# Fused gated cross-attention and attention block on one core: who issues the transfers that build the key stack

## What is computed

```
def reference(x, ctx, g_xattn, g_ffn, Wa, Wp, w_std, w_rec):
    xq = quant_dequant_act_1x128(layernorm(x))
    wq = quant_dequant_weight_128x128(ctx)
    x = x + tanh(g_xattn[0]) * einsum('emk,enk->emn', xq, wq)
    fused = layernorm(x) @ (Wa * col_scale)          # Q, K (32 columns a head), V
    scores = einsum('bhtd,bhsd->bhts', Qf, Kf) * scale, causal
    y = einsum('bhts,bhsd->bhtd', softmax(scores), V)
    return x + tanh(g_ffn[0]) * (y @ Wp)
```

## Time and profile before

| | us |
|---|---|
| median of 3 runs (513.59 to 514.74) | 514.0 |
| the profiled execution | 513.52 |
| its span, first to last instruction | 511.5 |
| TensorE busy, 87% of the span | 443.2 |
| VectorE busy, 65% | 331.8 |
| ScalarE busy, 53% | 273.6 |
| GpSimd busy, 28% | 145.2 |

### The profile page before, as it was taken

One profiled execution on the slowest core, in us unless ns is written; L12 is line 12 of the kernel. 1 busy time (PEld: TensorE's weight loads), 2 busy tenths in 40 slices (PEclk: granted clock), 3 DMA queues, 4 the chain that ended last, 5 costly groups with the idle time before them and its releaser, 6 DMA issues.

```text
span 511.5 us, 7890 instructions
## 1 busy us (share of the span) xinstructions
PE 443.2 (87%) x2536; PEld 319.0 (62%) x2536; DVE 331.8 (65%) x1110; ACT 273.6 (53%) x530; POOL 145.2 (28%) x264
## 2 busy tenths in 40 slices
PE   0366886999878999999888999999788999999995
PEld 0244665776544788776555788776455788666763
DVE  4789624588997243688998243678995255565535
ACT  2886226687446542687455552588556333454430
POOL 5667435233214300233214400233222101121110
PEclk9999998999999999999989999999999999999999
DMA  6402154414420244314420244414310243332102
GB/s 227 184 1 84 42 186 97 104 37 99 104 78 1 63 104 140 119 36 100 102 86 3 53 97 120 143 38 99 89 27 2 69 101 88 93 96 72 55 9 82
DMA packets 28024, 42.61 MB, mean 83 GB/s; under 512 B 8272, under 2 KB 8528, under 8 KB 27984
## 3 DMA queue, kind: packets, MB, share of 16 engines
q1 hardware_dynamic: 26448, 41.97, 29.4%
q10 hardware_dynamic: 1536, 0.14, 0.2%
HBM read 12.59 MB, written 4.19 MB: 33 GB/s over the span
## 4 chain that ended last, share of the span: by engine, by line
PE 57%; DVE 15%; ACT 12%; SPq 6%; DMA 4%; issue 2%; POOL 2%; ACTq 1%; POOLq 0%; DVEq 0%
PE pv_bank L731 8%; PE mm_bank L579 7%; PE mm_bank L581 7%; PE mm_bank L580 7%; PE exp_bank L717 5%; SPq L387 5%; DVE x_all L1205 5%; PE max_bank L700 4%; DVE max_bank L1234 4%; ACT work L1005 3%; PE mm_bank L758 2%; PE mm_bank L759 2%; PE mm_bank L760 2%; PE turn_bank L595 2%; DMA col_root<-in_L_ffn_w_rec 2%
## 5 line engine op out<-in xcount | busy, mean ns | idle before, releaser
L1234 DVE CUSTOM_DVE_ANT_0 max_bank<-max_bank,causal 128x512 f32<-128x512 f32 (+3 forms) x256 | 118.9, 516 | 46.9 <-PE max_bank L700 46.9
L495 POOL TENSOR_SCALAR_AFFINE_SELECT work<-work 128x384 f32<-128x384 f32 x64 | 33.5, 524 | 285.4 <-ACT work L1005 285.4
L1005 ACT ACTIVATE work<-exp_bank 128x512 f32<-128x512 f32 (+1 forms) x192 | 91.5, 525 | 39.9 <-PE exp_bank L717 39.5
L731 PE MATMUL pv_bank<-work,v_aug 128*33 128x256 f32 (+3 forms) x512 | 75.2, 436 | 0.0
L700 PE MATMUL max_bank<-k_stack,q_stack 96*128 96x512 f32 (+3 forms) x256 | 61.7, 336 | 12.0 <-DVE row_max L1234 6.0
L717 PE MATMUL exp_bank<-q_stack,k_stack 97*128 97x512 f32 (+3 forms) x256 | 66.5, 351 | 3.6 <-DMA q_stack<-neg_max 1.9
L1217 DVE SCALAR_TENSOR_TENSOR qk_lo<-mm_bank,col_root,qk_hi 128x512 fp32r<-128x512 f32 x32 | 24.0, 749 | 61.3 <-ACT qk_hi L978 61.2
L1205 DVE SCALAR_TENSOR_TENSOR x_all<-mm_bank,coef,x_all 128x128 f32<-128x128 f32 x224 | 60.4, 340 | 2.5 <-PE mm_bank L627 2.5
L700 PEld LDWEIGHTS max_bank<-k_stack,q_stack 96*128 96x128 f32 x256 | 45.3, 192 | 22.7 <-DVE row_max L1234 10.1
L731 PEld LDWEIGHTS pv_bank<-work,v_aug 128*33 128x33 f32 x512 | 27.4, 110 | 47.2 <-issue 40.4
L717 PEld LDWEIGHTS exp_bank<-q_stack,k_stack 97*128 97x128 f32 x256 | 43.7, 191 | 16.2 <-ACT work L1005 4.3
(11 more groups left out here) (161 smaller groups left out, 794.1 us busy)
## 6 DMA issues: line engine op xcount, KB each, us to landing
q_stack<-qk_hi SPq DMA_DIRECT2D x128, 64.0 KB, 2.0
k_stack<-qk_hi SPq DMA_DIRECT2D x128, 64.0 KB, 2.0
x_all<-in_x SPq DMA_DIRECT2D x16, 256.0 KB, 4.1
ctx_raw<-in_ctx SPq DMA_DIRECT2D x16, 256.0 KB, 3.8
q_stack<-qk_lo SPq DMA_DIRECT2D x64, 64.0 KB, 2.0
k_stack<-qk_lo SPq DMA_DIRECT2D x64, 64.0 KB, 2.0
out<-x_all SPq DMA_DIRECT2D x16, 256.0 KB, 2.2
work<-in_L_ffn_Wa SPq DMA_DIRECT2D x3, 768.0 KB, 9.4
```

What stands on the lines that cost most here:

```text
L495: pool.affine_select(out=three, in_=three, compare_op=ALU.is_ge, fill=0.0, base=0, pattern=[[0, 3], [1, P]], channel_multiplier=-1)
L731: last = pe.matmul(pv_bank[64 * j:64 * j + D + 1, P * m:T], v_aug[:, m, 2 * u + j, :], prob[j][:, PROB_COL[m]:PROB_COL[m] + T - P * m], st ...
L1005: act.activation(prob[j][:, UNIT_COL[k]:UNIT_COL[k] + UNIT_LEN[k]], exp_bank[(3 * j + k) % 2][:, 0:UNIT_LEN[k]], ACT.Exp, scale=SCALE).the ...
L1234: last = dve.tensor_tensor_reduce(max_bank[unit % 2][:, col:col + width], max_bank[unit % 2][:, col:col + width], causal[:, T - width:T], ...
```

## The change

SyncE keeps the six transfers of each step that build the query stack. The six that build the key stack are issued by GpSimd from a new function `stack_k`, with a semaphore per slot of their own, `s_kstack`; both engines use a common helper `stack_rows`. TensorE and ScalarE, which waited for 192 counts of `s_stack`, wait for 96 of each. GpSimd's calls stand at fixed places of its program: four in `POOL_FIRST`, step 4's at the head of step 2, step 5's behind step 2's zeroing, those of steps 6 and 7 behind step 3's, and the four for the next batch at the batch's end. Nothing of the arithmetic changes.

```
-POOL_FIRST = "i0 s0 s1 s2 s3 o0 s4 s5 s6 l0 l1 s7 l2 l3 r0 j0 j1 j2 r1 j3 g0 g1 g2 g3 p0"
+POOL_FIRST = "i0 s0 s1 s2 s3 o0 s4 s5 s6 l0 l1 s7 l2 l3 r0 j0 j1 j2 r1 j3 k0 k1 g0 g1 g2 k2 k3 g3 p0"
...
+K_STACKS = {2: (5,), 3: (6, 7)}
...
+        s_kstack = [sem(f"s_kstack{i}") for i in range(SLOTS)]
...
+        def stack_rows(eng, u, w, dst, parts, done):
+
+            g, s = u // 2, u % SLOTS
+            for j in range(2):
+                rows = slice(D * (2 * (u % 2) + j), D * (2 * (u % 2) + j) + D)
+                for a, part in enumerate(parts):
+                    eng.dma_start(dst[D * a:D * a + D, s, j, :].bitcast(FP32),
+                                  part[rows, g % 2, w, :].bitcast(FP32)).then_inc(done[s], 16)
...
-                for dst, w, parts in ((q_stack, 0, (qk_hi, qk_lo, qk_hi)), (k_stack, 1, (qk_hi, qk_hi, qk_lo))):
-                    sp.wait_ge(s_qklo, 8 * n + 2 * g + w + 1)
-                    for j in range(2):
-                        rows = slice(D * (2 * (u % 2) + j), D * (2 * (u % 2) + j) + D)
-                        for a, part in enumerate(parts):
-                            sp.dma_start(dst[D * a:D * a + D, s, j, :].bitcast(FP32),
-                                         part[rows, g % 2, w, :].bitcast(FP32)).then_inc(s_stack[s], 16)
-
+                sp.wait_ge(s_qklo, 8 * n + 2 * g + 1)
+                stack_rows(sp, u, 0, q_stack, (qk_hi, qk_lo, qk_hi), s_stack)
...
+            def stack_k(n, u, first=False):
+
+                if not first:
+                    pool.wait_ge(s_st, 48 * n + 6 * (u - SLOTS) + 6)
+                pool.wait_ge(s_qklo, 8 * n + 2 * (u // 2) + 2)
+                stack_rows(pool, u, 1, k_stack, (qk_hi, qk_hi, qk_lo), s_kstack)
...
+                elif kind == "k":
+                    stack_k(0, i, first=True)
...
                 for u in range(STEPS):
+                    if u == 2:
+                        stack_k(b, 4)
                     fill(POOL_GAPS[u][0])
                     zero_future(b, u, 0)
                     fill(POOL_GAPS[u][1])
                     zero_future(b, u, 1)
+                    for v in K_STACKS.get(u, ()):
+                        stack_k(b, v)
                     fill(POOL_GAPS[u][2])
+                if more:
+                    for v in range(SLOTS):
+                        stack_k(n, v)
...
-                    pe.wait_ge(s_stack[s], 192 * (2 * n + u // SLOTS + 1))
+                    pe.wait_ge(s_stack[s], 96 * (2 * n + u // SLOTS + 1))
+                    pe.wait_ge(s_kstack[s], 96 * (2 * n + u // SLOTS + 1))
...
-                        act.wait_ge(s_stack[s], 192 * (2 * n + g // 2))
+                        act.wait_ge(s_stack[s], 96 * (2 * n + g // 2))
+                        act.wait_ge(s_kstack[s], 96 * (2 * n + g // 2))
```

## The result

| | us |
|---|---|
| median before, measured alongside (4 runs, 512.93 to 514.74) | 513.8 |
| median after (4 runs, 547.02 to 555.63) | 552.1 |
| ratio, 95% interval | 1.066, 1.062 to 1.071 |
| the profiled execution after; its span | 548.9; 546.8 |

The ratio leaves disturbed runs out, so it lies nearer to the profiled execution than the median does; 1.0664 of 513.8 is a loss of 34 us. The direction held, and the range (547 to 655) by 1 us, since 1.0664 of 513.8 is 547.9. The forecast of 605 did not: it had the loss at 91.6 us, more than twice the measured one.

What follows compares the result with a forecast made beforehand. TensorE held 57% of the chain of waits, SyncE's queue 6%. Terms of 19.4 + 55.2 + 7.0 + 4.0 + 6 = 91.6 us added to 513.5 gave 605 us, range 547 to 655.

Steps and rivals of the forecast that it cites:

- c = 1.0: Assumed price in us of one transfer issue on GpSimd; the sum moves by 120 us per us of it.
- rival 1: An issue on GpSimd costs what it costs SyncE, 0.635 us; 562 us in all, chance 0.19.
- start: Batch 0's start: twelve issues delay g0, twelve more delay g3, its cast and step 0's negation; +19.4 us.
- step 2: Batches 0 to 2: six issues for step 4 stand ahead of scaling u0, delaying ScalarE's cast; +7.7 us each.
- step 3: Batches 0 to 2: step 5's transfers sit between causal zeroing and u2, whose cast already waited; +6.0 us each.
- step 4: Batches 0 to 2: 12 issues, r0 and two zeroings come before TensorE's weighted values; +4.7 us each.
- last batch: Twelve issues and two zeroings end after TensorE needs them, with short steps not covering the issues; +4.0 us.
- batch ends: After g3, six issues and a landing finish later than TensorE reads that stack; +3.5 us, twice.
- the clock: Six idle times of 6 to 8 us at steps 2 and 3 each bring slow clock costing about 1; +6 us.
- Rival 2: Issuing on GpSimd is nearly free, up to 0.4 us an issue; 520 to 545 us, chance 0.07.
- Rival 3: GpSimd's issues are held up by VectorE, an issue costing above 1.4 us; 725 us at 2.0, chance 0.07.
- Rival 4: Faster: SyncE's queue was the bound and GpSimd had room; 507 us, chance 0.03.

Runs made afterwards that it cites:

- the run with halves: Each key transfer of the changed kernel split into two of 256 columns, so GpSimd issues 12 per step; 607.4 us, ratio 1.181.
- g3 early: Against the changed kernel, GpSimd scales g3 before issuing the key transfers of steps 2 and 3; 542.7 us, ratio 1.056.
- u0 early: Against the changed kernel, u0 and u1 are scaled in step 2 before step 4's key transfers; 535.4 us, ratio 1.041.
- the covered kernel: Against the changed kernel, all key transfers stay on GpSimd but none stands ahead of a scaling ScalarE waits for; 516.4 us, ratio 1.006.

## Why the prediction was right and wrong

**The price of an issue was mis-sized, and that is the failure.** "I take c = 1.0: the work moves to the engine whose row says 1.04, and each row of a transfer has 512 elements too." It measured 0.49 to 0.51, inside the band of 0.4 to 0.8 that the prediction gave to rival 1. The argument took an instruction's length for work on elements, and the run with halves, 256 columns instead of 512, shows that the elements of a row don't enter. The nearer row was SyncE's issue, the same instruction on another engine; the rival built on it (562 us) deserved more than its 0.19, and it too was too dear. My own steps, worked again with 0.49, give 7.2 for the start, 3 x 4.64 for step 2, 3 x 2.94 for step 3, nothing for step 4 and the last batch (4.7 - 6.1 and 4.0 - 6.1 are below zero), 2 x 0.44 for the batch ends and 6 for the clock: 36.8, so 550.3 us, against the 548.9 of the profiled execution and a median of 552.1. Of the 91.6 forecast, 55 were the price. The slope of 120 us per us of c would have given 544; it runs on below zero where a term has ended. That the sum with the right price comes within 2 us of the profiled execution is in part luck too: step 3 was 8.8 us too dear in it, and the five other terms of the table below together 6.9 too cheap.

| term | forecast at 1.0 | by the same steps at 0.49 | measured, profiled run |
|---|---|---|---|
| start | 19.4 | 7.2 | 8.2 |
| steps 0 and 1 | 0 | 0 | 0.5 |
| step 2, three batches, with its slow clock | 23.1 + 3 | 13.9 + 3 | 19.5 |
| step 3, three batches, with its slow clock | 18.0 + 3 | 8.8 + 3 | 3.0 |
| step 4, three batches | 14.1 | 0 | 0 |
| batch ends | 7.0 | 0.9 | 2.1 |
| last batch | 4.0 | 0 | 1.6 |

*Start: right in mechanism and size.* 8.2 against 7.2; part of the difference is the first two issues, which took 1.27 us (at 70.96) where the later pairs took 0.99. The run with g3 early takes it all away, and with halves it was 19.9 against 19.4.

*Step 2: right.* The cast C0 comes 4.66 us later than the step's start explains (125.20 against 111.57 + 8.97), where 4.64 come out of my steps. It is 4.66 and 4.65 in the batches 1 and 2. The rest of the 6.3 is the clock, as I read it. From C0 to the next negation the kernel took 8.63 us before (111.57 to 120.20) and 10.31 after (125.20 to 135.51), 1.7 more, with TensorE at 0.50 for the 4.5 us shown and ScalarE waiting 1.40 us for TensorE's product at the end of it. In the batches 1 and 2 it was 1.3 and 2.6 more. I had put 1 us to each of six idle times, and three of these come to 5.6. In step 3 the clock fell in batch 2 alone (0.57 from 392 to 396), the batch with the 1.9 us.

*Step 3: wrong in how much of it counts.* "The cast of u2 was already waiting 0.70 us for GpSimd, so it all counts." A wait in front of an instruction does not make it critical. The cast did come later, by 1.95 us (2.65 against 0.70), yet step 4's negation moved by 0.4 us only. Behind the cast ScalarE had waited for TensorE, in its timeline before the change:

```profile
123.39 0.60 ACT L1001 ACTIVATE values<-pv_bank 97x512 f32<-97x512 f32 x1 [0.41 <-PE pv_bank L731]
...
125.60 0.60 ACT L942 ACTIVATE wt_lo<-turn_bank 128x512 fp32r<-128x512 f32 x1 [0.64 <-PE turn_bank L595]
...
128.64 0.60 ACT L942 ACTIVATE wt_lo<-turn_bank 128x512 fp32r<-128x512 f32 x1 [0.74 <-PE turn_bank L595]
```

and the engine that was full there was VectorE, in the stretches of the steps 3 and 4 before the change (busy PE, PEld, DVE, ACT, POOL):

```profile
122.00:130.00 8.00, 6.97 (x60) 4.90 (x54) 7.70 (x31) 6.18 (x12) 1.08 (x3) 1.00 0.39 94
130.00:142.00 12.00, 9.81 (x61) 5.97 (x60) 11.90 (x50) 5.53 (x12) 4.00 (x12) 1.00 0.50 132
```

Those waits of ScalarE, 1.79 us together, are slack that absorbed the cast's delay: after the change the first two are gone and the third is 0.40. That reading fits the other batches and kernels. In the changed kernel the cast of u2 waits 2.65, 3.00 and 4.13 us and step 3 costs 0.4, 0.7 and 1.9; with u0 early it waits 3.56 and 3.58 and step 3 costs 1.3 and 1.3 in the batches 0 and 1. Each time some 2.2 to 2.3 us of the wait are absorbed, the 0.70 that was there before among them. It is not a constant: 1.0 in batch 2 with u0 early, and 1.5, 2.3 and 1.5 with twice the issues. With twice the issues step 3 cost 3.4 to 3.9 us where the full shift was 6, and taking u2 out from behind the issues gained nothing in all.

*Step 4: right where it could be seen.* At 0.5 us GpSimd is back in time. With halves TensorE waits 4.13, 4.35 and 5.01 us for the zeroing in step 4 and 3.21 in the last batch, the wait that the prediction named with 4.7 and 4.0, and the lateness grows by 5.1, 4.1 and 6.6 us from step 4's negation to step 7's.

*Batch ends and last batch: not explained by my steps.* 2.1 against 0.9, and 1.6 against nothing. The 1.6 is TensorE's two waits for the negated maxima shown with the covered kernel, a landing that the prediction had left out; the batch ends I did not trace.

*The rivals.* Rival 2 (nearly free) needed issues up to 0.4. Rival 3, issues held up by VectorE, is out: the middle one of 192 takes 0.498 us and the longest 0.763, with VectorE busy for 61% of the span. The Trainium skill (SBUF — State Buffer, the box on VectorE blocking DMA) may hold for the two-port modes that it names; no row here tells whether one ran. Rival 4, the faster kernel, named the right place: the runs with u0 early and with all covered show that without the order around step 2 the loss goes, but no gain of 6 us appears even then. The kernels with g3 early gain 0.7 us at step 0's negation, which there follows the cast of g3 without a pause: ScalarE's row of casts was the next bound behind TensorE's two waits.
The Trainium skill (DMA: Bandwidth & Descriptors, Specifications) has GpSimd's first byte some 0.4 us later than SyncE's, by its 1 and 0.6 us. The landings agree in sign, 2.4 us against 2.0. It is a latency and not the time for which the engine is held, which was 0.50 us on GpSimd and 0.635 on SyncE: the other way round.

## What to carry to other kernels

An idle share says nothing about where an in-order engine can take a task: look at the instruction that will stand right behind it, who waits for that, and put the task after it; here the order of two scalings and six issues was worth 13 us. Price a moved instruction by the same instruction on another engine, not by that engine's arithmetic, and if no row has it, settle the price with one small run first. Before a delay counts in full, look at the waits of the same engine behind it: they are slack until another engine's full stretch says otherwise. And a small transfer that an engine waits for can land later when many transfers are moved beside it; here it is, as I read it, what is lost in the last batch, 1.3 to 1.6 us.

## What I had not expected of the hardware

GpSimd issued a transfer between places of SBUF in 0.50 us, less than SyncE's 0.635, and for 32 KB as for 64 KB; only the landing goes by the size (1.7 against 2.4 us). The first transfer after a wait took up to 0.76. TensorE's granted clock stood at 0.50 after idle times of 8.2 and 4.3 us alike, and in the stretch shown behind one of 1.53. ScalarE's transfer of 4 KB took 4.3 us to land where it had taken 2.7 or less.
